# Mixing four branches of a gated attention layer: the products and sums move from GpSimd to VectorE

## What is computed

```python
stats = concatenate([_per_head_stats(local_short), _per_head_stats(local_long),
                     _per_head_stats(delta_out), _per_head_stats(v_direct)], -1)
h1 = gelu(concatenate([hs_exp, stats], -1) @ mlp1_w.T + mlp1_b)
p = softmax((h1 @ mlp2_w.T + mlp2_b) / softplus(logit_temp), -1)
p = maximum(p, 0.02); p = p / sum(p)
o = p[..., 0:1] * local_short + p[..., 1:2] * local_long + p[..., 2:3] * delta_out + p[..., 3:4] * v_direct
o = o + sigmoid(conv_res_logit) * local_short
o = _rmsnorm(o, norm_w)
o = o.reshape(b, l, H * DV) @ o_w.T
```

## Time and profile before

| | |
|---|---|
| median of 3 runs | 3349.95 us (3346.38 to 3358.67) |
| the profiled execution | 3352.05 us, of which the span is 3350.3 us |
| VectorE busy over the span | 1880.1 us, 56% |
| GpSimd busy over the span | 768.1 us, 23% |
| stage `gate1` | about 2838 to 3041 us, 203 us |
| VectorE, GpSimd busy in the stage | 167.36 us, 136.31 us |

### The profile page before, as it was taken

One profiled execution on the slowest core, in us unless ns is written; L12 is line 12 of the kernel. 1 busy time (PEld: TensorE's weight loads), 2 busy tenths in 40 slices (PEclk: granted clock), 3 DMA queues, 4 the chain that ended last, 5 costly groups with the idle time before them and its releaser, 6 DMA issues. The chain is left out here.

```text
span 3350.3 us, 45498 instructions
## 1 busy us (share of the span) xinstructions
PE 2567.9 (77%) x16281; PEld 1561.7 (47%) x16281; DVE 1880.1 (56%) x3568; ACT 1314.2 (39%) x2778; POOL 768.1 (23%) x960
## 2 busy tenths in 40 slices
PE   2328888899999999822999999466698775676991
PEld 1114444355555555411444444344586664345881
DVE  4348887566766666444333333359765665992333
ACT  2216666455655555521333333434101211552331
POOL 1241111355555555400000000000000000673330
PEclk8659999899999999955999999568656766777996
DMA  2121110100000000021300000213433110123552
GB/s 57 57 72 27 35 38 21 32 4 4 4 4 4 1 4 1 1 86 35 71 17 0 17 7 0 81 51 94 122 119 76 41 39 13 44 48 126 178 183 83
DMA packets 197701, 159.06 MB, mean 47 GB/s; under 512 B 55546, under 2 KB 180205, under 8 KB 197053
## 3 DMA queue, kind: packets, MB, share of 16 engines
q1 hardware_dynamic: 184506, 142.83, 15.5%
q0 software_dynamic: 4544, 9.35, 0.8%
q10 hardware_dynamic: 8448, 4.20, 0.4%
HBM read 112.16 MB, written 49.35 MB: 48 GB/s over the span
## 5 line engine op out<-in xcount | busy, mean ns | idle before, releaser
L1285 DVE TENSOR_TENSOR x_hg<-x_h,x_g_ps 128x512 f32<-128x512 f32 x248 | 170.5, 688 | 329.2 <-PE x_y_ps L1230 297.0
L940 ACT ACTIVATE a_p<-a_s_ps,a_nmax 128x512 f32<-128x512 f32 (+3 forms) x512 | 266.7, 546 | 99.8 <-DVE a_nmax L854 99.8
L1270 ACT ACTIVATE x_h<-x_h_ps,x_w 128x512 f32<-128x512 f32 x256 | 175.8, 687 | 323.7 <-PE x_g_ps L1226 296.2
L854 DVE TENSOR_REDUCE a_nmax<-a_s_ps 128x2 f32<-128x1024 f32 (+3 forms) x256 | 204.8, 821 | 138.6 <-PE a_s_ps L755 133.8
L1222 PE MATMUL x_h_ps<-x_anT,x_w 128*128 128x512 f32 x512 | 263.2, 597 | 25.2 <-DMA x_gT<-gT_d 24.7
L912 POOL TENSOR_SCALAR a_p<-a_p,a_rden 128x512 f32<-128x512 f32 (+3 forms) x512 | 262.6, 532 | 13.0 <-DVE a_rden L861 12.9
L1230 PE MATMUL x_y_ps<-x_hg,x_w 128*128 128x512 f32 x496 | 253.1, 592 | 0.0
L554 DVE TENSOR_REDUCE a_shift<-a_s_ps 128x2 f32<-128x1024 f32 (+3 forms) x256 | 202.0, 819 | 54.0 <-PE a_s_ps L461 51.9
L951 ACT COPY a_e<-a_pt_ps 128x1024 f32<-128x1024 f32 (+3 forms) x256 | 174.5, 713 | 109.6 <-PE a_pt_ps L768 109.6
L619 ACT ACTIVATE a_e<-a_s_ps 128x1024 f32<-128x1024 f32 (+1 forms) x192 | 166.0, 884 | 109.3 <-PE a_s_ps L461 109.1
L768 PEld LDWEIGHTS a_pt_ps<-ident,a_p 128*128 128x128 f32 x1280 | 146.8, 141 | 126.2 <-issue 66.2
(11 more groups left out here) (438 smaller groups left out, 5307.1 us busy)
## 6 DMA issues: line engine op xcount, KB each, us to landing
f_w<-in_wgud SPq DMA_DIRECT2D x39, 768.0 KB, 4.3
l_band<-in_fir_long SPq DMA_DIRECT2D x16, 768.0 KB, 4.7
parts_d<-p_parts SPq DMA_DIRECT2D x16, 384.0 KB, 2.5
a_qs<-parts_d SPq DMA_DIRECT2D x96, 64.0 KB
a_ks<-parts_d SPq DMA_DIRECT2D x96, 64.0 KB
sorted_d<-in_fill SPq DMA_DIRECT2D x1, 5031.0 KB, 27.9
f_xr<-sorted_d SPq DMA_DIRECT2D x39, 129.0 KB, 4.2
g_row<-hs_d SPq DMA_DIRECT2D x64, 64.5 KB, 2.0
```

The lines of the kernel that those rows point to most:

```text
L854: last = nc.vector.tensor_reduce(nmax[g % 4][:, 2 * at:2 * at + 2], s_ps[g % 2][:, :, c:c + width(i)], AX.X, ALU.max, negate=True)
L940: last = nc.scalar.activation(p[g % 4][:, h, c:c + width(i)], s_ps[g % 2][:, h, c:c + width(i)], ACT.Exp, bias=nmax[g % 4][:, col], accum_ ...
L1270: nc.scalar.activation(h[q][:, :], h_ps[q][:, :], ACT.Gelu, bias=weights(i * SLOTS + c, slice(2 * P, 2 * P + 1)))\
L1285: nc.vector.tensor_tensor(hg[q][:, :], h[q][:, :], g_ps[q][:, :], ALU.mult).then_inc(hg_ready, 1)
```

## The change

The seven mixing instructions leave GpSimd's program and join VectorE's as a new step `mixed(i-1)` at the end of round i, behind `normed(i-2)`. They are the same four products and three sums on the same tiles, but grouped so that only three of the seven are followed by a wait. GpSimd is left with the memset and the 64 scatters, now without any wait between the portions but that for the row's load. The last instruction of `shares` (L2347) no longer raises `pr_ready` but is a `step`, so it is followed by a wait; the wait of `shares` for `o_ready` is gone.

```diff
         def _(gp):
-            step = Chain(gp, pool)
...
                 sent += SPREADS[b]
-                out = o[b % 2]
-                gp.wait_ge(pr_ready, b + 1)
-                after(gp, on_ready, b - 1)
-                after(gp, osq_ready, b - 1)
-                share = lambda i: bc(pr[b % 2][:, :, i], CH, 2)
-                step(nc.gpsimd.tensor_tensor(groups(out[:, :]), branch(b, 0), share(0), ALU.mult))
-                for i in range(1, 4):
-                    step(nc.gpsimd.tensor_tensor(groups(term[i % 2][:, :]), branch(b, i), share(i), ALU.mult))
-                    last = nc.gpsimd.tensor_tensor(out[:, :], out[:, :], term[i % 2][:, :], ALU.add)
-                    if i < 3:
-                        step(last)
-                last.then_inc(o_ready, 1)
...
             def shares(b):
                 p = pr[b % 2]
                 v.wait_ge(ez_ready, b + 1)
-                after(v, o_ready, b - 1)
...
-                nc.vector.tensor_tensor(p0, p0, bc(res[:, :], NB), ALU.add).then_inc(pr_ready, 1)
+                step(nc.vector.tensor_tensor(p0, p0, bc(res[:, :], NB), ALU.add))
+
+            def mixed(b):
+                out, share = o[b % 2], lambda i: bc(pr[b % 2][:, :, i], CH, 2)
+                after(v, osq_ready, b - 1)
+                nc.vector.tensor_tensor(groups(out[:, :]), branch(b, 0), share(0), ALU.mult)
+                step(nc.vector.tensor_tensor(groups(term[1][:, :]), branch(b, 1), share(1), ALU.mult))
+                nc.vector.tensor_tensor(groups(term[0][:, :]), branch(b, 2), share(2), ALU.mult)
+                step(nc.vector.tensor_tensor(out[:, :], out[:, :], term[1][:, :], ALU.add))
+                nc.vector.tensor_tensor(groups(term[1][:, :]), branch(b, 3), share(3), ALU.mult)
+                step(nc.vector.tensor_tensor(out[:, :], out[:, :], term[0][:, :], ALU.add))
+                nc.vector.tensor_tensor(out[:, :], out[:, :], term[1][:, :], ALU.add).then_inc(o_ready, 1)
...
                 if i >= 2:
                     normed(i - 2)
+                if 1 <= i <= B:
+                    mixed(i - 1)
```

## The result

The changed kernel takes 3416.41 us (median of 4 runs, 3415.01 to 3417.47), the kernel before 3351.69 us on the same chip (4 runs, 3346.38 to 3358.67). The ratio is 1.0192, with a 95% interval of 1.0172 to 1.0211. So it is 65 us slower, where 3 us were forecast.

A forecast was written before the change was run, and what follows sets the result against it. VectorE was taken to bound settled rounds. Up to the last L2323, 28.3 us added less 23.8 given back made +4.5; the last chain's 1.8 less left +2.7 us, about 3353 us, range 3345 to 3363.

The forecast's parts named there:

- What is added: VectorE: seven mixing instructions for each sequence, 4.6 us (bounds 4.3 to 5.4); L2347's new wait costs 0.10 us.
- rival 3: VectorE's products with a share are dear, read in steps of four: 17 us more, 3370 us; chance 0.05.
- What is given back: VectorE without GpSimd's mixing, per settled round: subtractions 1.84 us, `on` 1.36, L2352 0.39, L2319 0.21.
- rival 2: VectorE gets nothing back, as its long instructions have another cause: 3378 us; chance 0.03.
- rival 1: Scatters take over GpSimd's part in the collision with VectorE in rounds 0 to 3: 15 us, 3368 us; chance 0.05.
- The tail: Chain from the last shares to the last square, mixing now on VectorE: 7.7 us instead of 9.5, 1.8 us less.
- The last wait: VectorE's wait for the network's result of the last sequence: about 3.2 us shorter, 4.3 us instead of 7.51.
- The sum: Whole span: 4.5 us later up to the last L2323, 1.8 us less in the last chain, +2.7 us.
- The scatters: GpSimd's 64 scatters without pauses, 0.96 + 0.30 us each, end after 81 us, near 2927 us.
- GpSimd's queue: Scatters without pauses: ending earlier brings nothing; meeting more whole-tile VectorE instructions costs at most 2.4 us.
- New waits: Waits at L2328, L2317 and for `mixed`: no added cost, with the chain through PE and ScalarE unchanged.
- something unnamed: Any outcome outside the forecast and the listed rivals, counted as slower by over 0.5%; chance 0.03.

The follow-up runs named there:

- Run 12: Changed kernel with GpSimd held until the mixed tile is ready, scatters in runs of 20 with pauses of 20 to 37 us: 3359.62 us, ratio 1.0020.
- run 1: Changed kernel, but GpSimd waits for `o_ready` after each portion of scatters, computing nothing: 3353.08 us, ratio 1.0005 to the kernel before.
- run 4: Changed kernel with a GpSimd memset of 128x512, waited for, behind each scatter (one in 1.8 us): 3365.91 us, one execution.
- run 2: Kernel before, mixing still on GpSimd, with all 64 scatters in one run ahead of the mixing of sequence 0: 3411.2 us.
- run 9: Changed kernel with a first run of 40 scatters, the rest in small portions behind waits for the mixed tile: 3388.42 us, ratio 1.0106.
- run 16: Changed kernel with six GpSimd memsets of 128x512, each waited for, behind every 16th scatter: 3358.08 us, ratio 1.0017.
- run 15: Changed kernel with a short GpSimd memset (128x32), waited for, behind each scatter (1.38 us apart): 3370.55 us, ratio 1.0064.
- run 8: Changed kernel with VectorE doing `variances(i)` ahead of `logits(i-1)` in its rounds: 3418.7 us.
- run 10: Changed kernel with ScalarE, in VectorE's place, copying the network's result out of PSUM: 3421.78 us, ratio 1.0205.
- run 11: Changed kernel with 8 parts of small matmuls in a round in place of 32 (one matmul of 16 columns per head): 3393.44 us, ratio 1.0121.
- run 5: Changed kernel with 48 row buffers loaded ahead, so 48 scatters run without a load beside them: 3404.0 us.
- run 13: Changed kernel with 16 parts of small matmuls in a round in place of 32 (two matmuls of 8 columns per head): 3404.58 us, ratio 1.0159.
- run 3: Changed kernel with 40 one-column memsets at the head of VectorE's program of the stage, shifting its code: 3415.01 us.
- run 6: Changed kernel with 56 transposes of the identity at the head of TensorE's program of the stage, shifting its code: 3414.69 us.
- run 7: Changed kernel with 16 transposes of the identity at the head of TensorE's program of the stage, shifting its code: 3421.71 us.
- run 14: Changed kernel with each scatter replaced by a plain transfer of the same rows from the same queue: 3355.38 us, ratio 1.0012.

## Why the prediction was wrong

Most of its steps held:

- **What is added:** a mixing of 4.6 us was forecast and 4.59 measured. Products with a share cost what sums do (rival 3 falls).
- **What is given back:** the subtractions take 1.90 and 0.69 us, `on` 0.69 and 0.69, everywhere (rival 2 falls). The round is 22.90 us; 22.9 was forecast. The changed kernel itself says little on rival 1, as VectorE stood still beside most scatters. Run 12 decides it: the mixing from 2929.55 us on lies beside scatters, and each of its seven takes 0.68 or 0.69 us.
- **The tail:** from the last of the shares to the last square were to be 7.7 us and are 3094.59 - 3086.87 = 7.72. The last wait was to be 4.3 us and is 4.27, which is in part luck. The forecast took TensorE's chain to be as long as before, and it was, with the same granted clock of 0.68 while the hidden matmuls ran (5.40 us for the eight in both). In run 1 the clock was 1.00 there, its upper level throughout, the eight took 3.70 us and the wait was 2.58; in run 4 it was 0.54 in the mean, they took 6.77 us and the wait was 6.49. The prediction has no term for this.
- **The sum** of +2.7 us: from VectorE's first sums to the end of the last copy the stage took 192.48 us before and 251.66 (2851.02 to 3102.68) in the changed kernel, 59.18 more. Without the 56.44 us that the wait of round 1 has grown, 2.74 are left. In run 1 it is 2.1 us, with a last wait 1.7 us shorter by that clock.
- **The scatters** were to take 81 us and take 2930.57 - 2848.69 = 81.9.

**The step that failed** is "GpSimd's queue": "earlier scatters bring nothing". It asked only when the scatters end, and whether they disturb VectorE's instructions, not what a row of 64 without a pause does while it runs. And under "New waits" it held "the chain through PE and ScalarE is unchanged". None of the four rivals had it; it fell under "something unnamed", at 0.03. The longest row of scatters in the kernel before was 12, some 15 us, so its trace could not show it; the queue was to run in a way of which no row spoke, and its bounds (0 to 2.4 us) came from rows with pauses. The change took away the mixing, which had also been the pause. The account: the wait at round 1 went from 1.33 to 57.77 us, 56.4 us, where the prediction had nothing; the rest of the stage is 2.7 us longer; and the stage began 2.9 us later in this profiled execution (first scatter at 2848.69, before at 2845.76). Together 62.1, of the 62.9 us between the spans.

**What is shown and what isn't.** Shown: the loss needs the scatters close together (runs 1, 2, 4, 9, 16; run 15 is the edge); it is TensorE's results that are held, whoever reads them (runs 8, 10, 11); TensorE's parts then go one in 2.1 to 2.8 us (runs 5, 8, 11, 13); the place of the code (3, 6, 7) and the loads (5) aren't what makes it. Likely and not shown: that the transfers must be indirect (run 14, where GpSimd also rests). That something fills up a little faster than it is carried off, and is cleared by a few microseconds without scatters, fits runs 4, 15 and 16 but was not seen itself. Run 12 doesn't fit it if scatters alone fill it: behind the long pause the hold came sooner. It would fit if TensorE's parts filled it too (run 5 points the same way), which no run tests. What it is stays open. One path that no run shuts out is the recording itself: each execution here has a span for its core, so all were recorded. The traces give no sign of it: no record of TensorE is missing, with 16281 recorded parts before, after and in every run that leaves TensorE's program as it is. The Trainium skill (NOTIFIC — the notification-queue block, Overflow: three behaviours, one of which stalls the engine) says that the block that writes the records holds its producers back inside, and that this can throttle an engine. No run here can show whether that is the path, nor whether an execution without records would stop.

## What to carry to other kernels

Work that is taken off an engine may have been the pause of what stands behind it in the queue: when a change makes a queue run closer than any row shows, keep its spacing (one wait for each portion, as in run 1, or a few microseconds of idling once in 16, as in run 16), or measure the close run by itself first. When all engines stop together, look at which result the first of them waits for, and at what the one busy engine is doing. A stop whose length changes with the number of instructions of the engine that is waited for tells a pace, and not a latency.

## What the runs showed of the hardware that was not expected

- Scatters of 128 rows issued 1.26 us apart held what TensorE's matmuls report, from some point between 17 and 28 us after the first; its parts of matmuls then went one in 2.1 to 2.8 us, and all was free 1 to 9 us behind the last scatter. At 1.38 us apart the time depended on the execution (3357 to 3388 us), at 1.8 us there was no stop in the one execution taken. Plain transfers of the same rows from the same queue, one in 0.9 us on average with pauses between them, made no stop.
- Scatters hardly lengthened VectorE's two-input instructions of 128x512 (0.68 to 0.69 us for most beside them, 0.74 for some), and some of its small scalings more (0.40 against 0.22 us in run 1). Waits of 0.5 to 1.2 us between its own instructions came up in such a stretch (run 11).
- TensorE's records can show matmuls as ended 56 us before their semaphore reaches anyone. The profile's name for the releaser is then no guide: "remote" in most waits, and a transfer of another stage in run 11.
